# Two graph layers on one core: GpSimd in place of VectorE adds the new rows of the first layer's last ten pairs of units

## What is computed

```python
h = relu(layernorm(x))
c = concat(h[src], h[dst], relation_embedding[type]) @ W1 + b1
b = leaky_relu(c @ w2, 0.01)
alpha = softmax of b over the edges with the same dst
x = x + leaky_relu(segment_sum(c * alpha, dst), 0.01)      # first layer

h = relu(layernorm(x))
agg = segment_sum(h[src], dst)
x = x + where(a node has edges, agg, h)                    # second layer
```

## Time and profile before

| | us |
|---|---|
| median of 3 runs | 1811.62 (1809.88 to 1812.3) |
| profiled execution, its own time | 1812.44 |
| its span, first to last instruction | 1807.6 |
| DVE busy in the span | 1538.6 (85%) |
| PE busy | 1489.1 (82%) |
| ACT busy | 1373.4 (76%) |
| POOL busy | 1231.9 (68%) |
| mean granted TensorE clock | 0.952 |

### The profile page before, as it was taken

How to read it: one execution, slowest core, us unless ns; L and a number is a source line. 1 busy time by engine, 2 the same in 40 slices (tenths; PEclk the granted TensorE clock), 3 DMA queues, 4 the chain that set the end, 5 groups by cost and what they waited for, 6 DMA issues and landing times.

```text
span 1807.6 us, 37626 instructions
## 1 busy us (share of the span) xinstructions
PE 1489.1 (82%) x12132; PEld 1349.5 (75%) x12132; DVE 1538.6 (85%) x5561; ACT 1373.4 (76%) x3555; POOL 1231.9 (68%) x1069
## 2 busy tenths in 40 slices
PE   1489999999999999999999962677767767776767
PEld 0489999999999999999999952555555555555556
DVE  5768999999999999999999686788878888788886
ACT  0578888888888888888888723677777777787777
POOL 4778877677767776777774007777777777777772
PEclk9999999999999999999999986799999999899998
DMA  6455666566666666665665563566766766666543
GB/s 147 123 137 153 171 169 167 170 168 166 169 169 169 167 169 170 169 168 169 169 171 138 154 196 88 143 193 179 195 177 194 197 178 186 184 190 185 160 109 117
DMA packets 465338, 297.91 MB, mean 165 GB/s; under 512 B 32123, under 2 KB 434357, under 8 KB 465142
## 3 DMA queue, kind: packets, MB, share of 16 engines
q1 hardware_dynamic: 430390, 243.09, 48.4%
q0 software_dynamic: 34752, 52.43, 11.5%
HBM read 208.14 MB, written 104.34 MB: 173 GB/s over the span
## 4 chain that ended last, share of the span: by engine, by line
PE 52%; ACT 11%; DVE 10%; POOL 9%; DMA 9%; issue 7%; POOLq 0%; SPq 0%; DVEq 0%; ACTq 0%
POOL xe L962 9%; DMA xe<-x_d,idx_t 8%; PE c_p L1316 7%; ACT cs L1242 6%; PE c_p L1317 6%; PE t_p L1304 6%; PE c_p L1321 5%; PE c_p L1319 5%; ACT cs L1245 4%; PE y_p L1342 4%; PE t_p L1303 3%; PE t_p L1306 3%; PE t_p L1305 3%; PE y_p L1344 3%; PE y_p L1345 3%
## 5 line engine op out<-in xcount | busy, mean ns | idle before, releaser
L962 POOL DMA_INDIRECT xe<-in_x,idx_t x522 | 680.9, 1304 | 255.2 <-issue 153.3
L962 POOL DMA_INDIRECT xe<-x_d,idx_t x522 | 531.7, 1019 | 268.8 <-issue 137.1
L1011 DVE BATCH_NORM_STATS2 st<-xn 128x6 f32<-128x128 f32 x1566 | 349.7, 277 | 157.5 <-DMA xe<-x_d,idx_t 132.2
L1242 ACT ACTIVATE cs<-xn,nbias,rstd 128x128 f32<-128x128 f32 x783 | 326.2, 479 | 54.4 <-DVE nbias L1055 54.4
L1242 ACT ACTIVATE an<-xn,nbias,rstd 128x128 f32<-128x128 f32 x783 | 326.9, 483 | 16.5 <-DVE nbias L1055 16.5
L1013 DVE BATCH_NORM_STATS2 st<-xe 128x6 f32<-128x128 f32 x1044 | 243.4, 274 | 0.0
L1268 ACT ACTIVATE lr<-y_p 128x390 f32<-128x390 f32 x261 | 129.6, 497 | 137.3 <-PE y_p L1345 131.8
L1245 ACT ACTIVATE ae<-xe,nbias,rstd 128x128 f32<-128x128 f32 x522 | 226.2, 482 | 0.0
L1245 ACT ACTIVATE cs<-xe,nbias,rstd 128x128 f32<-128x128 f32 x522 | 225.2, 478 | 0.0
L1316 PE MATMUL c_p<-w1a,th 128*128 128x129 f32 x1044 | 216.1, 289 | 0.0
L1317 PE MATMUL c_p<-w1b,th 128*128 128x129 f32 x1044 | 202.6, 276 | 0.0
(11 more groups left out here) (176 smaller groups left out, 3478.8 us busy)
## 6 DMA issues: line engine op xcount, KB each, us to landing
xn<-in_x SPq DMA_DIRECT2D x130, 384.0 KB, 6.5
x_d<-xn SPq DMA_DIRECT2D x130, 384.0 KB, 7.5
xn<-x_d SPq DMA_DIRECT2D x130, 384.0 KB, 4.2
out<-xn SPq DMA_DIRECT2D x130, 384.0 KB, 3.8
plr<-place_d SPq DMA_DIRECT2D x65, 256.0 KB, 3.6
tyr<-types_d SPq DMA_DIRECT2D x65, 256.0 KB, 5.6
xe<-in_x,idx_t POOLq DMA_INDIRECT x522, 3.8
xe<-x_d,idx_t POOLq DMA_INDIRECT x522, 3.5
```

The costliest lines, as they stand in the source:

```text
L962: nc.gpsimd.indirect_dma_start(out=xe_of(L, u)[:, e, :], out_offset=None, in_=a, in_offset=bass.IndirectOffsetOnAxis(ap=idx_t[:, j:j + 1], ...
L1011: v.bn_stats(st[:, j % 2, UN * at + i, :], xs_of(L, u)[:, i, :])
L1242: a(own[:, i, :], xs_of(L, u)[:, i, :], ACT.Relu, bias=nbias[:, j % 2, c:c + 1], scale=rstd[:, j % 2, c:c + 1])
```

## The change

For pairs 121 to 130 the add of `lr` to `xn` is taken out of DVE's queue and put into POOL's. `DRAIN = (NU - LAG) // 2 + 2` is 121, and `range(DRAIN, PAIRS)` has ten members (the change was announced as eleven pairs). POOL has the ten adds behind its last gather of the first layer and ahead of its wait for the stores. Each waits for `own` (the pair's leaky relu is done) and for a new semaphore `none` (the pair's `none_t` has read `lr`), and counts up `x1` as DVE's did. DVE keeps L1153 and L1161 for these pairs. `pair_of` moves up so that both engines can use it.

```diff
+            DRAIN = (NU - LAG) // 2 + 2
...
                 for u in range(NU):
                     gather(L1, x, u)
+                for i in range(DRAIN, PAIRS):
+                    n, xs = pair_of(L1, i)
+                    at = 2 * i % 4
+                    y = lr[:, at:at + n, :, :].rearrange("p u i c -> p (u i) c")[:, :, 0:D]
+                    pool.wait_ge(L1.own, i + 1)
+                    pool.wait_ge(L1.none, i - DRAIN + 1)
+                    nc.gpsimd.tensor_tensor(xs, xs, y, ALU.add).then_inc(L1.x1, 1)
                 for n in range(NQ - XS, NQ):
                     pool.wait_ge(stored.of(n), stored.count(n))
...
-                    v.tensor_scalar(none_t[:, 2 * UN * i:2 * UN * i + UN * n], y[:, :, D + 1], 0.5, None, ALU.is_lt)
+                    last = v.tensor_scalar(none_t[:, 2 * UN * i:2 * UN * i + UN * n], y[:, :, D + 1], 0.5, None, ALU.is_lt)
+                    if i >= DRAIN:
+                        last.then_inc(L1.none, 1)
+                        return
                     dve.wait_ge(L1.own, i + 1)
                     v.tensor_tensor(xs, xs, y[:, :, 0:D], ALU.add).then_inc(L1.x1, 1)
```

More of the change, by code:

```diff
@@ L832, in __init__ @@
                     self.x1 = sem(f"x1_{n}")
+                    self.none = sem(f"none_{n}")
             L1, L2 = Layer(1), Layer(2)
@@ L887, in valid, with pair_of @@
                 return 0 <= u < NU
+            def pair_of(L, i):
+                n = min(2, NU - 2 * i)
+                at = 2 * i % QU * UN
+                return n, xn[:, (L.first_sb + 2 * i // QU) % XS, at:at + n * UN, :]
             block = ctx2.enter_context(nc.Block())
@@ L1139, in select @@
                     last.then_inc(L.sel, 1)
[L1141 to L1144, removed]
                 def slope1(i):
```

## The result

The changed kernel is slower: 1815.46 us median of 15 runs (1814.0 to 1818.38) against 1811.62 us, a ratio of 1.0022 with a 95% interval of 1.0014 to 1.003. The forecast was 1819.2 in a range of 1807 to 1823. The sign was right, the size forecast was twice the measured one: 7.6 us, where 3.8 were measured.

The account below looks back on a forecast made before the run. DVE's queue was taken to bound the first layer's drain. To pair 129 31.3 us in place of 24.74, then 4.05 in place of 3.02, made 7.6 us more: 1811.62 + 7.6 = 1819.2 us, range 1807 to 1823.

Parts of the forecast that it names:

- What bounds the kernel: End of first layer: DVE never rests from 1052.5 to 1080.3 us, each pair costing a 3.15 us turn of its queue.
- a microsecond more or less here is one in the total: Drain of the first layer: the second layer starts from its last store, so any change there reaches the total in full.
- Whether the work hides beside DVE: Drain: POOL's add doesn't hide under DVE's remaining 2.28 us but holds L1153 and L1135 for its whole length; chance 0.58.
- The argument from the speed of L1135: Drain: L1135 takes 0.323 us for 256 elements, so most likely runs at the double rate and can be held by POOL.
- T: Length of POOL's 128x768 add in the drain: taken as 1.6 us, with bounds 1.28 to 1.94.
- The short one: Last POOL add of the drain, 128x384: taken as 0.85 us.
- The handover: Each drain turn: 0.1 us lost between POOL's and DVE's instructions, on top of 2.28 + T.
- The tail: From the L1153 of pair 129 to the end of the last add: 4.05 us in place of 3.02.
- No contention: Rival, drain: the engines don't disturb each other, DVE's turn is 2.28 us, total 1807.1, 4.5 us faster; chance 0.17.
- only L1153 held: Rival, drain: L1135 runs free under POOL's add, a turn is 2.8 us, total 1810.8, about the same; chance 0.17.
- late first add: Rival, POOL's first add must be fetched: 3 to 5 us on top, 1823; chance 0.08, shared with a longer T.
- transfers close behind: Drain, no-contention case: 16.4 us of DMA work in 21.3 us would be full, limiting the gain to 3.5 to 5 us.

Follow-up runs that it names:

- spare add: Kernel before (DVE keeps all adds) plus a 128x768 POOL add on data nobody needs in each of the drain's ten turns: 1823.19 us.
- sel_on_act: Kernel before, with ACT building one of the two `sel` of each unit in the drain: 2058.07 us, ratio 1.0009 on a slower chip; repeated, 2057.43 us, 1.0021.
- The memset: Kernel before (DVE keeps all adds) plus a write-only 128x1920 POOL memset on data nobody needs in each of the drain's ten turns: 1819.64 us.

## Why the prediction was right, and what was mis-sized

**What bounds the kernel.** Right for this change: the drain's length went into the total. It grew by 4.63 us in the profiled execution, and the medians by 3.8. As a general statement (a microsecond more or less here is one in the total) it was too strong: of 13.3 us more in the kernel with the spare add 1.6 were given back before the first gather, and of the 2.87 less in sel_on_act 2.65.

**Whether the work hides beside DVE.** Right, and this gave the sign. The step from the earlier trace rows to "POOL's add holds L1153 and L1135" is what the traces show: a `sel` of 1.69 us and a leaky relu of 1.84 in place of 0.32 and 0.87. The memset and the spare add separate the two kinds: the mere writer held `sel` but not DVE's two-input add, the reader excluded both. With `row` in PSUM `sel` was free. The rule quoted from the Trainium skill, "SBUF — State Buffer", section "Who interferes with whom", agrees with all three in which instructions exclude each other (3.86, 4.64 and 2.75 us a turn). The argument from the speed of L1135 is borne out, though not by itself: read from PSUM it takes 0.45 in place of 0.32 and is not held. The 0.13 more are 0.51 ns an element, the difference between the two rates of the prediction (1.04 less 0.51, about). That the rate, and not the place it reads from, decides is supported by the gathers beside L1011 but not shown for POOL's add.

**T.** Taken 1.6 as the middle of wide bounds (1.28 to 1.94), measured 1.70. The Trainium skill's "GPSIMD Engine Reference", section 3.1, gave an estimated 1.7. The short one was 0.95 against 0.85.

**The handover, the term that was mis-sized.** I took T + 0.1 for the loss in a turn. It is 1.37 with T at 1.70: a held `sel` was over 0.08 us after POOL's add, not 0.32, so that all but 0.08 of its own time had run in the shadow of the add. With the leaky relu it is 0.13: it ended 0.74 behind the add in place of 0.87. The fault was to stack the two instructions end to end, where the rows already showed a handover below zero: in the earlier trace rows 0.09 is lost of 0.14 left and 0.44 of 0.48, and in the earlier trace rows the cast ends 0.28 behind the memset, less than the 0.41 that it takes alone. I rounded it to a cost of 0.1. `none_t` also fell from 0.12 to 0.07 us. A turn was 3.60, not 3.98; over seven turns that is 2.7 us too much. With T at its measured 1.70 the forecast turn would have been 4.08, so the short T hid part of the error.

**The tail.** Forecast 4.05 (its terms add up to 4.01), measured 5.11. I had eight `sel` groups held and the tail free. In fact behind pair 128 the two `sel` were over before POOL's add took hold, and it fell on the leaky relu of pair 129: from one leaky relu to the next only 2.10 us (0.44 of it idle), where the forecast has 3.34 (2.51 - 0.87 + 1.70), and then 0.97 more in the tail. Put together: 27.28 + 5.11 = 32.4 against the forecast 31.3 + 4.05 = 35.35. That the miss is no larger is in part luck: the turns were forecast too long, the tail and T too short.

**The rivals.** No contention asked for turns of 2.3, only L1153 held for 2.8: both fell at 3.60. The first add of POOL was as short as the rest (1.69) and began as soon, 0.32 us behind the start of `none_t`, so no late first add shows. My estimate of transfers close behind was of use: when the drain did get shorter, the stores gave part of it back.

## What to carry to other kernels

An engine that is idle in the profile isn't free: before moving work from DVE to POOL, look at what DVE runs beside it, and find rows where instructions of the two overlap (here a cast of 1.43 in place of 0.41). Where POOL's instruction held a DVE instruction here (one with two inputs in SBUF when POOL's reads SBUF too, or a `sel` with its row in SBUF), it cost DVE's queue about POOL's time less that of the held instruction: 1.37 us a turn, more than the 0.87 saved. Splitting POOL's instruction shrank that to 1.24, and giving `sel` its operand from PSUM took it away, at 0.13 us for each `sel`. And when a stretch gets shorter, look at once at the transfers queued behind its last step.

## What was not expected of the hardware

- A held DVE instruction isn't put off but covered: `sel` ended 0.08 us after POOL's add (0.32 alone), the leaky relu 0.74 after (0.87 alone). How much of this is work done while held, and how much the end of POOL's record lying behind the release, no run tells.
- Even an instruction on 3 elements is held: the last `none_t` had a record of 1.63 us in place of 0.16.
- An operand in PSUM makes the one-hot multiply slower (0.45 against 0.32 us) and the kernel faster beside POOL: 2.75 against 3.60 a turn.
